# A decoder layer with a mixture of experts on one core: 32 small transfers of row maxima issued by ACT instead of SP

## The reference, cut to what matters

```python
x = layernorm(x + self_attention(x))        # 16 heads of 8; Q, K, V and the output are circulant products plus bias
x = layernorm(x + cross_attention(x, ctx))  # similarity, two softmaxes, a product with a 512x128 matrix
x = layernorm(x + experts(x))               # top 2 of 8 experts and one shared expert, each 128 -> 512 -> 128
```

## Time and profile before

| what | value |
|---|---|
| median of 3 runs | 420.73 us (417.86 to 422.58) |
| the profiled execution, its own time | 423.07 us |
| its span | 421.3 us |
| busy: PE, DVE, ACT, POOL | 347.6, 281.5, 175.3, 194.0 us |
| granted TensorE clock, mean | 0.96 of full speed |

### The profile page before, as it was taken

How to read it: one execution, slowest core, us unless ns; L and a number is a source line. 1 busy time by engine, 2 the same in 40 slices (tenths; PEclk the granted TensorE clock), 3 DMA queues, 4 the chain that set the end, 5 groups by cost and what they waited for, 6 DMA issues and landing times.

```text
span 421.3 us, 8518 instructions
## 1 busy us (share of the span) xinstructions
PE 347.6 (82%) x2415; PEld 224.6 (53%) x2415; DVE 281.5 (67%) x834; ACT 175.3 (42%) x498; POOL 194.0 (46%) x377
## 2 busy tenths in 40 slices
PE   2637887888988879798967998978799999999880
PEld 1224466666656658576656554534455555555450
DVE  3435477777878897869876867987466666666322
ACT  2212344444534443344532344344355555555313
POOL 9700022224222558722474434357755656565323
PEclk9999999998999998969998799999899999999996
DMA  4764544766654732310003001113211111110063
GB/s 100 171 212 128 178 141 120 210 202 172 186 157 132 201 98 63 104 34 11 27 28 119 14 13 44 33 39 92 63 45 44 47 45 45 40 50 19 26 201 100
DMA packets 53197, 39.56 MB, mean 94 GB/s; under 512 B 7623, under 2 KB 46632, under 8 KB 53147
## 3 DMA queue, kind: packets, MB, share of 16 engines
q1 hardware_dynamic: 50881, 34.33, 29.3%
q0 software_dynamic: 2272, 4.69, 3.3%
HBM read 26.05 MB, written 12.69 MB: 92 GB/s over the span
## 4 chain that ended last, share of the span: by engine, by line
PE 42%; DVE 23%; issue 10%; POOL 9%; DMA 6%; SPq 5%; ACT 2%; ACTq 0%; POOLq 0%; DVEq 0%
PE pT L1491 7%; PE pS L1491 6%; DVE negmax L934 4%; PE pM L1502 4%; POOL xs L633 3%; PE pM L1297 3%; DVE inv_den L950 2%; POOL rstd L613 2%; PE pO L1482 2%; PE pT L1321 2%; PE pT L1492 2%; PE pS L1311 2%; PE pS L1492 2%; PE pO L1334 2%; DVE X L1004 1%
## 5 line engine op out<-in xcount | busy, mean ns | idle before, releaser
L711 POOL DMA_INDIRECT ys<-sim_rhs,row_dest x39 | 40.5, 1039 | 43.3 <-ACT sim_rhs L868 41.7
L766 ACT ACTIVATE PT<-pT 128x512 f32<-128x512 f32 x64 | 38.0, 594 | 33.3 <-PE pT L1321 29.9
L1491 PE MATMUL pT<-W,XH 128*128 (+1 forms) x94 | 51.7, 632 | 0.0
L934 DVE TENSOR_REDUCE negmax<-pS 128x4 f32<-128x512 f32 x64 | 43.4, 679 | 9.6 <-PE pS L1311 9.2
L1071 DVE TENSOR_TENSOR PT<-pT,PT 128x512 f32<-128x512 f32 x47 | 32.4, 689 | 25.9 <-PE pT L1492 17.7
L1491 PE MATMUL pS<-W,XH 128*128 (+1 forms) x94 | 49.3, 607 | 0.0
L611 POOL TENSOR_SCALAR vareps<-meanvar 128x1 f32<-128x1 f32 x32 | 8.4, 263 | 86.1 <-DVE meanvar L963 85.8
L1311 PE MATMUL pS<-Kdiag,Qst 128*128 128x512 f32 x64 | 40.4, 638 | 6.3 <-DMA Kdiag<-parts_scr 4.7
L852 ACT COPY XH<-pO 128x384 f32<-128x384 f32 x47 | 22.4, 478 | 49.4 <-PE pO L1484 45.7
L1502 PEld LDWEIGHTS pM<-W,XH 128*128 128x128 f32 x188 | 28.1, 191 | 21.0 <-issue 17.4
L633 POOL DMA_INDIRECT xs<-X,slot x32 | 33.2, 1036 | 8.1 <-issue 5.8
(11 more groups left out here) (264 smaller groups left out, 828.1 us busy)
## 6 DMA issues: line engine op xcount, KB each, us to landing
parts_scr<-qk_hi SPq DMA_DIRECT2D x16, 256.0 KB, 2.9
W<-in_L_ffn_w SPq DMA_DIRECT2D x16, 256.0 KB, 3.9
Qst<-parts_scr SPq DMA_DIRECT2D x32, 96.0 KB
Kdiag<-parts_scr SPq DMA_DIRECT2D x64, 48.0 KB
Kst<-parts_scr SPq DMA_DIRECT2D x32, 96.0 KB
Qdiag<-parts_scr SPq DMA_DIRECT2D x64, 48.0 KB
sim_add<-xs SPq DMA_DIRECT2D x39, 65.0 KB
parts_scr<-qk_lo SPq DMA_DIRECT2D x8, 256.0 KB, 3.0
```

The source lines that it names most:

```text
L711: pool.indirect_dma_start(ys.ap(), bass.IndirectOffsetOnAxis(ap=row_dest[:, k:k + 1], axis=0), YO[:, i % RING, :], None).then_inc(s_ysc[i ...
L766: act.activation(PT[:, u % 3, :], pT[:, 0, :], ACT.Exp, scale=SCALE).then_inc(p_sb, 1)
L934: dve.tensor_reduce(out=negmax[:, b % 2, HG * j:HG * (j + 1)], in_=pS[:, u % 2, :].rearrange("p (g k) -> p g k", g=HG), axis=AX.X, op=ALU.max,
L1491: pe.matmul(bank, XH[:, 1 - p, 2 * P:3 * P], W[:, bass.ds(e_up * I2, I2)], start=True, stop=False)
```

## The change

The function `max_rows` moves from SP's list to ACT's, with the same two waits and the same two DMAs. In a slot of the maxima ACT now does: the copy of the maxima, the exponential, the two DMAs, then step 5 and the logits. Since the DMAs write into Qdiag and nothing else on ACT had waited for POOL's clearing of it, ACT's list begins with a wait for c_pool (the second buffer clearing that is counted, L576) ahead of its first copy.

```diff
 # SP
-            def max_rows(b):
-
-                sp.wait_ge(mxT_sb, b + 1)
-                if b >= 2:
-                    sp.wait_ge(sT_ps, U * (b - 1))
-                for part in range(2):
-                    sp.dma_start(Qdiag[RQ + part:RQ + part + 1, b % 2, :, :, :].rearrange("p j g n -> p (j g) n").bitcast(F32),
-                                 maxT[H * part:H * (part + 1), b % 2, :]).then_inc(s_maxrow[b % 2], 16)
...
             for n in range(FIRST_SLOT, LAST_SLOT + 1):
-                if n >= -3 and n % U == 1 and (n + 3) // U < B:
-                    max_rows((n + 3) // U)
 # ACT
+            def max_rows(b):
+
+                act.wait_ge(mxT_sb, b + 1)
+                if b >= 2:
+                    act.wait_ge(sT_ps, U * (b - 1))
+                for part in range(2):
+                    act.dma_start(Qdiag[RQ + part:RQ + part + 1, b % 2, :, :, :].rearrange("p j g n -> p (j g) n").bitcast(F32),
+                                  maxT[H * part:H * (part + 1), b % 2, :]).then_inc(s_maxrow[b % 2], 16)
...
                 if 0 <= n < U * B:
                     exps(n)
+                if n >= -3 and n % U == 1 and (n + 3) // U < B:
+                    max_rows((n + 3) // U)
                 for b, k in late:
                     chain(b, k)
...
+            act.wait_ge(c_pool, 2)
             act.wait_ge(c_ident, 2)
             act.copy(ident_r[:], ident[:]).then_inc(c_identr, 1)
```

## The result

The changed kernel took 422.32 us (median; 419.33 to 425.94), the one before, in the same comparison, 419.42 us (417.86 to 423.18): ratio 1.006, 95% interval 1.0031 to 1.0088. By the ratio that is +2.5 us (the two medians alone are 2.9 us apart) where +1.2 us was forecast: within 1%, and inside the range. A later comparison gave 1.0061 (1.0017 to 1.0104). The loss is small but it is there. The forecast had its direction right; but one step of the working was wrong, and what that step left out is about as large as the whole loss.

The account below looks back on a forecast made before the run. No engine is full; a PE - DVE - POOL - DVE - PE round of handovers once a batch sets the attention stage's pace. 423.07 + 2.0 - 0.82 = 424.3 us, in the median's terms 420.73 + 1.2 = 421.9 us; range 417.6 to 426.8.

Parts of the forecast that it names:

- Part 3: Start: ACT's first copy waits for POOL's clearing, XT ends near 11.6 us, 0.4 us of cover remains; cost 0.
- L1297 waiting for XT: Sign of being wrong at the start: PE's first projection would wait for XT instead of starting at 12.1 us.
- Part 2: ACT's two DMA issues between exponential and step 5 delay batt_col and hqT, then POOL's vareps; cost 2.0 us.
- D: Delay of batt_col, hqT and the logits in a batch from ACT issuing the pair of DMAs; taken as 0.80 us.
- Part 1: SP loses 32 issues, mostly slack; PE's waits in slots 24 and 25 go, gaining 0.82 us (bounds 0 and 2.09).
- Part 4: The 32 DMAs of 8 KB land 2.1 us after issue but are needed three slots later; no cost.
- Issue in order: Rival, chance 0.2: ACT's DMAs start only after the exponential ends, D is 1.26 us; 425.7 us, slower by 1.2%.
- A shared generator: Rival, chance 0.13: SP's and ACT's transfers are generated one at a time, adding 4.2 us with no gain; 424.9 us.
- SP's relief decides: Rival, chance 0.22: hqT's delay is absorbed in the batch, waits of slots 24 and 25 count fully; -2.09 us, 418.6 us.

Follow-up runs that it names:

- e2: Kernel before with only the new wait for the clearing of Qdiag ahead of ACT's first copy, maxima DMAs still on SP; ratio 1.0066.
- e11: Changed kernel with the wait moved to ACT's first DMA of maxima, a repeat of e1 beside the changed kernel; 425.20 us, ratio 1.0036.
- e8: Kernel before without the 32 DMAs of row maxima and the waits for them, so without subtracting the maxima before the exponential; ratio 0.9959.
- e3: e1 with ACT's two DMAs of maxima moved behind step 5 and the copy of the logits; ratio 0.9992.
- e6: e1 with ACT's two DMAs of maxima one slot later, behind step 6 and ahead of step 2; ratio 0.9993.
- e4: e1 with POOL doing the root (vareps and rstd) ahead of hq_x, DMAs left where the change puts them; ratio 0.9992.
- e7: e1 with two more 8 KB DMAs, writing to an unused array, issued by ACT behind each pair of maxima; ratio 1.0372.
- e9: e3 with e4's edit: maxima DMAs behind the copy of the logits and POOL's root ahead of hq_x; ratio 1.0002.
- e1: Changed kernel with the wait for the clearing of Qdiag moved from ACT's first copy to its first DMA of maxima; ratio 1.0012.

## Why the prediction was right, and where it was not

**Part 3, the wait at the start: wrong, and the step that failed.** "So 0.4 us of cover is left, and the wait costs nothing." The term was 0; the trace shows 2.36 us (L1295 at 11.61 against L1294 at 9.25), e2's ratio 2.8 us (1.3 to 4.3), the changed kernel beside e11 1.7. The prediction read the wait of L1297, "for circ", as cover for XT. It asked who reads XT, not who waits on the semaphore of its copy. L1294 does, by `projections_free()`, and circ hangs on L1294. Of the 3.6 us by which XT is late, 1.3 were hidden: XT had been ready at 7.94 and PE started L1294 at 9.25 for another reason, which the trace calls "issue". It is the load of the matrix that L1294 multiplies, issued at 4.90. Its row in the view of the DMAs of before (KB, then us from issue to landing):

```profile
W<-circ_scr SPq DMA_DIRECT2D x1, 256.0 KB, 4.3
```

4.90 + 4.3 = 9.2, and PE starts at 9.25. In the ten profiles without a wait at the head the landing takes 3.9 to 5.2 us, and PE starts this product about 0.1 us after it each time, at 8.90 to 10.17. With the wait it starts at 11.61 in all three. So the wait's price at this place is 1.4 to 2.7 us, depending on the execution; the 2.36 are one sample of it. The sign that the prediction named ("L1297 waiting for XT") would never have shown, since the wait moved one instruction up.

**Part 2, ACT's issuing: right in the mechanism, the place and the size of a batch.** D was to be 0.80 and was 0.84. The periods were to grow by 0.33 us in batches 4 and 5 and grew by 0.34 and 0.32. In the second profile of the changed kernel the periods from 3, 7 and 12 grew by 0.56, 0.32 and 0.36 us, where 0.33, 0.56 and 0.14 stood in the sum. For batch 6, before is no measure, since its waits of slot 24 and 25 lie there; e8, which has neither these waits nor the delay, and a like dip of the clock, has 10.41 us there, and so has the changed kernel: nothing, where 0.33 stood. And the period from 10 is 0.19 shorter (11.80 or 11.81 us in all four profiles with the pair ahead of step 5 and the old order on POOL, against 12.00 or 12.01 in before, e2, e3, e6 and e8), which nobody forecast and no run explains. Together that is 1.7 us against the forecast's 2.0; that the single terms were off and their sum so near is in part luck. By ratios it is 1.3 us with wide intervals. e4 shows that most of it goes the way named, e7 that the place is the one named.

Two of the named signs of being wrong do show, if faintly: the longest issue in the first profile takes 0.72 us, where 0.7 was the limit, and in batch 3 PE waits for hqT. There SP issues beside ACT, and batt_col comes 1.73 us behind the exponential:

```profile
64.41 0.38 PE L1400 MATMUL pX<-batt_col,X 128*128 128x1 f32 x2 [0.61 <-ACT hqT L785]
```

In batch 4 that wait is 0.17 us, later gone. Whether it adds anything to the path through POOL isn't shown.

**Part 1, SP's relief: right for the execution it was read from, short for the kernel.** The two waits cost 0.98 us, 0.82 were taken, so weighing PE's idle by DVE's came out well in this pair of profiles. Over many executions e8 gives 1.7 us. "In no other slot did PE wait for it" was true of that trace and not of the kernel: e2 waits in slots 5 and 8. And the other part of Qdiag, for which nothing was counted in slot 24, still holds PE up for 0.22 us there in the second profile of the changed kernel.

**Part 4, the transfers: right.** They land 2.7 us after issue (median), and in neither profile of the changed kernel does PE wait for them. But there is little to spare: in e9, behind the logits, those of batch 6 held PE up for 0.53 us, and in e6, issued one slot later, for 1.32 us:

```profile
101.09 0.47 PE L1327 MATMUL pT<-Qdiag,Kst 128*128 128x512 f32 x1 [1.32 <-DMA Qdiag<-maxT]
```

**The sum.** Forecast 2.0 - 0.8 + 0 = +1.2. Measured for parts 1 and 2 together +1.0 (mean of e1 and e11), with the start's 1.7 to 2.8 on top: 2.7 to 3.8, where the change itself measured +2.5 and +2.6, the one to 1.2 and the other to 1.8 us. What makes the loss clear of noise is the term that the prediction set at 0; parts 1 and 2, on which its sign rested, are by themselves not told from no change by any ratio. So that a loss was measured at all, and within the range, owes something to luck.

**Issue in order** fell: the pair starts 0.12 us after the exponential starts, not when it ends. The Trainium skill's page "Perfetto Trace Analysis" (DVE / Act Engine Instruction), by which the sequencer is free once it has pushed a compute instruction, agrees with that row.

**A shared generator** is seen by half. In the second profile of the changed kernel ACT's 16 pairs take 1.15 to 1.25 us, so ACT doesn't wait there as that rival wanted. SP's four issues of Qdiag take 1.54 to 1.58 us in six of the nine groups that have no pair of ACT beside them (1.81, 2.51 and 3.36 in the others), and 2.10, 1.84, 2.04, 1.81, 1.59, 1.59 and 2.02 in the seven that have. Groups of 2.8 us stand in the kernel before as well, without ACT. The cleanest is the last of the seven, in the slots of the maxima of batch 10. Here it is before, and then in that profile:

```profile
140.72 1.59 SPq L450 DMA_DIRECT2D Qdiag<-parts_scr  x4
```

```profile
143.08 2.02 SPq L450 DMA_DIRECT2D Qdiag<-parts_scr  x4
```

It takes 2.02 us in all five profiles that have ACT's pair ahead of step 5 (the changed kernel twice, e1, e11, e4), and 1.59 in the four that have no pair of ACT beside it (before, e2, e6, e8). So SP does lose part of what it was relieved of. And in batch 3 of e1, e3 and e4 ACT is held as well. In e1, SP's row and ACT's:

```profile
61.80 1.81 SPq L384 DMA_DIRECT2D X<-in_x  x1
```

```profile
61.77 1.83 ACTq L765 DMA_DIRECT2D Qdiag<-maxT  x2
```

Both end at the same time, as they do in e3 and e4 to 0.02 us, and the second issue of ACT's pair takes 1.23 to 1.47 us. What holds them both isn't shown. The Trainium skill's "DMA: Bandwidth & Descriptors" (Issuing engines are not separate DMA queues) says that a second issuing engine saves only the time of the sequencer; no row here speaks against it.

**SP's relief decides** fell with the sign, though e8 shows that about its 2 us exist (1.7). They are met by about as much delay on ACT. The versions without that delay and without the head's wait come to 0.999 to 1.000, and none of their intervals excludes no change. So no version here is shown to be faster than the kernel before.

## What to carry to other kernels

A DMA issued from a compute engine holds up that engine's next instruction for the whole of its issuing (here 0.6 us each as a rule, up to 1.5), even where it overlaps the one before: put it where the next instruction has that much room, or count what hangs on it. When a wait is added at the head of an engine's program, follow every instruction that signals behind it, and for each ask who waits on its semaphore, bank-free waits included, not who reads its result. And a wait that stands in one profile of a queue that is often late is a sample: size it from several executions, or from a version without the cause.

## What the runs showed of the hardware

- ACT's load of its tables ran at 0.79 us in the kernel before and at 3.62 in the changed kernel and e2, both with the new wait at the head: only when the identity matrix is there, which the first copy waited for before too (timeline of ACT, changed kernel). It costs nothing here, since it ends at 4.90 and POOL's clearing at 10.74:

```profile
3.62 1.28 ACT L879 ACT_TABLE_LOAD   x1 [3.62 <-POOL ident L558]
```

- In the four profiles in which ACT issues no DMA in the slot of the maxima (before, e2, e6, e8) the period of batch 4 is 10.71 or 10.72 us, while their spans run from 420.6 to 425.0 us. A period read away from the clock's dips is a far finer instrument than the span.
- The same load of 256 KB at the start (into W, L391 in the kernel before) took 3.9 to 5.2 us to land over all profiles. In the ten where PE's product with it didn't wait for XT, PE's start moved with it, from 8.90 to 10.17: more than a us of difference between two executions, before the attention stage begins.
- Two queues that issue at the same time can hold each other up: SP's group of four took 2.02 us beside ACT's pair and 1.59 without, and single issues of ACT and SP stretched together to 1.2 to 1.8 us.
- The place of a DMA issue changes its price many times over: 32 more on SP cost 5.1 us (2.7 to 7.4), 32 more on ACT between the exponential and batt_col 14.8 us.
